# Four batches of self attention written out one after another, each with its neighbours' projections and output between its steps

## What is computed

```
z  = rmsnorm(layernorm(x)) * ln1
kv_d, q_d = z @ kv_d_w, z @ q_d_w                      # 512 -> 128 each
k  = [kv_d @ k_u_w | rope(z @ rope_k_w)]               # 16 heads of 16 + 16
q  = [q_d @ q_u_w  | rope(q_d @ rope_q_w)];  v = kv_d @ v_u_w
P  = softmax(q k^T / sqrt(32), causal)                 # per head, 512 x 512
h  = layernorm(x) + (P v) @ o_w
hn = rmsnorm(h) * ln2
logits = hn @ router_w + router_b                      # 7 experts, the best 2
sum  table <- x + h                                    # written to DRAM, like hn ("rows")
slot table <- token and weight at each chosen expert's next places
```

## Time and profile before

| | |
|---|---|
| Median of 3 runs | 2096.5 us (2091.77 to 2099.65) |
| The profiled execution | 2092.79 us |
| Its span, first to last instruction | 2091.0 us |
| Mean granted TensorE clock | 0.875 |
| TensorE busy | 1733.6 us, 83% |
| VectorE, ScalarE, GpSimd busy | 65%, 50%, 43% |
| `front` without `cross` | about 95 to 791 us |

### The profile page before, as it was taken

One profiled execution on the slowest core, in us unless ns is written; L12 is line 12 of the kernel. 1 busy time (PEld: TensorE's weight loads), 2 busy tenths in 40 slices (PEclk: granted clock), 3 DMA queues, 4 the chain that ended last, 5 costly groups with the idle time before them and its releaser, 6 DMA issues. The chain is left out here.

```text
span 2091.0 us, 34098 instructions
## 1 busy us (share of the span) xinstructions
PE 1733.6 (83%) x9086; PEld 1287.2 (62%) x9087; DVE 1355.9 (65%) x2635; ACT 1037.8 (50%) x1967; POOL 900.1 (43%) x655
## 2 busy tenths in 40 slices
PE   4589879887988984999994794079999999999992
PEld 3456556564655653776772673068888888778881
DVE  6645525544635544667775655069999999899992
ACT  1144234324414423666661110068888888888880
POOL 5100110001011012244441377747888888887881
PEclk9599979988989986999996555579999999999996
DMA  8000000010010016357556213248788888898778
GB/s 293 0 1 1 21 22 2 1 41 3 1 41 1 1 41 172 102 140 181 104 89 183 81 42 90 55 113 203 162 190 195 173 174 190 200 230 198 129 126 271
DMA packets 128910, 222.88 MB, mean 107 GB/s; under 512 B 17536, under 2 KB 60416, under 8 KB 127072
## 3 DMA queue, kind: packets, MB, share of 16 engines
q0 software_dynamic: 52624, 113.84, 28.0%
q1 hardware_dynamic: 76176, 107.71, 15.8%
HBM read 143.74 MB, written 84.18 MB: 109 GB/s over the span
## 5 line engine op out<-in xcount | busy, mean ns | idle before, releaser
L1300 DVE TENSOR_TENSOR moe_w_lo<-moe_w_up,moe_w_hi 128x1536 fp32r<-128x1536 f32 (+1 forms) x216 | 408.4, 1891 | 35.1 <-ACT moe_w_hi L1186 34.4
L1186 ACT ACTIVATE moe_w_hi<-moe_w_up 128x1536 fp32r (+3 forms) x216 | 343.2, 1589 | 19.1 <-SPq L1088 19.1
L1127 POOL DMA_INDIRECT moe_rows<-moe_rows,moe_ids x200 | 319.4, 1597 | 68.1 <-issue 56.7
L1395 PE MATMUL psum<-moe_w_hi,moe_rows_hi 128*128 128x384 f32 (+1 forms) x864 | 323.4, 374 | 16.7 <-DVE moe_rows_lo L1294 16.7
L1396 PE MATMUL psum<-moe_w_lo,moe_rows_hi 128*128 128x384 f32 (+1 forms) x864 | 304.4, 352 | 0.0
L1397 PE MATMUL psum<-moe_w_hi,moe_rows_lo 128*128 128x384 f32 (+1 forms) x864 | 304.2, 352 | 0.0
L1421 PE MATMUL psum<-moe_w_down,moe_hid_t 128*128 (+1 forms) x544 | 268.7, 592 | 1.8 <-DVE moe_tail_t L1288 1.2
L599 POOL TENSOR_TENSOR prob<-x_sb,v_sb 128x512 f32<-128x512 f32 x16 | 20.2, 1265 | 475.2 <-DVE v_sb L738 475.2
L1143 POOL DMA_INDIRECT moe_sum<-moe_res,moe_ids x100 | 165.0, 1650 | 98.5 <-ACT moe_res L1223 55.1
L1143 POOL DMA_INDIRECT moe_other<-moe_res,moe_ids x100 | 165.9, 1659 | 89.3 <-ACT moe_res L1223 34.1
L851 PE MATMUL psum<-k_t,q_t 128*128 128x512 f32 (+3 forms) x512 | 184.2, 471 | 21.1 <-issue 15.8
(11 more groups left out here) (263 smaller groups left out, 3129.1 us busy)
## 6 DMA issues: line engine op xcount, KB each, us to landing
moe_w_up<-in_L_ffn_w_gate SPq DMA_DIRECT2D x32, 384.0 KB, 4.6
moe_w_up<-in_L_ffn_w_up SPq DMA_DIRECT2D x32, 384.0 KB, 5.8
moe_w_down<-in_L_ffn_w_down SPq DMA_DIRECT2D x32, 256.0 KB, 6.2
moe_w_down<-in_L_ffn_w_down SPq DMA_DIRECT2D x64, 128.0 KB, 6.6
moe_sum<-prob SPq DMA_DIRECT2D x4, 1024.0 KB, 4.2
moe_rows<-prob_t SPq DMA_DIRECT2D x4, 1024.0 KB, 4.5
moe_rows<-moe_rows POOLq DMA_DIRECT2D x16, 256.0 KB, 7.1
moe_other<-moe_res POOLq DMA_DIRECT2D x16, 256.0 KB
```

What stands on the lines that cost most here:

```text
L1127: pool.indirect_dma_start(rows[u][:, :], None, d["rows"], bass.IndirectOffsetOnAxis(ids[:, t:t + 1], 0)).then_inc(gathered[u], 16)
L1186: sc.activation(w_hi[u % SPLITS][:, :], w_up[:, bass.ds(at * DC, DC), :].rearrange("p a n -> p (a n)"), ACT.Copy).then_inc(T["wh"], 1)
L1300: v.tensor_tensor(w_lo[u % SPLITS][:, :], w_up[:, bass.ds(at * DC, DC), :].rearrange("p a n -> p (a n)"), w_hi[u % SPLITS][:, :].bitcast(F ...
L1395: mm(ps[:, 2 + i, 0:2 * I], hi, w_h, start=(k == 0), stop=False)
```

## The change

Loops are gone: every stream is written out for all four batches, with one running step number n = 32 b + s. Queries, keys, values and attended results have two sets of buffers (b % 2); `h` has its own memory, and x + h is written over x. The first norm is computed two batches ahead, in steps 24 to 27, and again in part at the residual. `attention` of b now has at each of its steps a piece of `between(b, s)`: norm turns, down, plain, rotary and value projections of batch b+1, and output, second norm, hidden turns, logits, choice and slots of batch b-1. For this `QUERY_ORDER` is (1, 0, 3, 2): the first 16 steps are narrow. A narrow step's two scores share one bank (0 or 1), so banks 2, 3 and 5 are free for the pieces. The queries are stored like the keys, q_t[128, 4, 512]; a head's score contracts over its own 32 rows, and both heads of a step now lie in the same group of 32. In `attend` the loop over heads is the outer one. ScalarE copies q (one pass instead of four), k and q_d, the latter two from VectorE. `take` waits until the bank's former content has been read. Cut to its core:

```diff
-QUERY_ORDER = (3, 0, 2, 1)
+QUERY_ORDER = (1, 0, 3, 2)
...
+        ends = lambda n: STEPS[n % NS][1] == HEADS // 2 - 1
+        is_wide = lambda n: STEPS[n % NS][0] >= 2
+        nth = lambda i: QUERY_ORDER.index(i)
+        BANK = {"zt": (2, 5, 2, 5), "kvd": 2, "qd": 5, "v": (2, 2, 2, 5), "pp": (5, 5, 2, 5), "hnt": (5, 2, 5, 2),
+                "tq": (5, 5, 2, 2), "tk": (2, 2, 5, 5)}
+
+        def head(hp, e):
+
+            return GH * (2 * (hp // GH) + e) + hp % GH
+
+        def score_at(n, e, cols):
+
+            u = n % 2
+            return ps[:, 2 * u + e, 0:cols] if is_wide(n) else ps[:, u, e * 256:e * 256 + cols]
...
+            def take(bank, name, n):
+
+                if bank in emptied:
+                    pe.wait_ge(S[emptied[bank][0]], emptied[bank][1])
+                emptied[bank] = (name, n)
 
...
+            def scores(n):
+                b, s = divmod(n, NS)
+                i, hp = STEPS[s]
+                cols = (i + 1) * P
+                if s == 0:
+                    pe.wait_ge(S["qts"], TPB * (b + 1))
+                    pe.wait_ge(S["kts"], TPB * (b + 1))
+                if s == 1 and n >= NS:
+                    pe.wait_ge(S["pexp"], 2 * (n - 3) + 2)
+                elif n >= 2 and not is_wide(n):
+                    pe.wait_ge(S["pexp"], 2 * (n - 2) + 2)
+                for e in range(2):
+                    if is_wide(n):
+                        if not is_wide(n - 1):
+                            pe.wait_ge(S["pexp"], 2 * (n - 2 + e) + 2)
+                        elif not is_wide(n - 2):
+                            take(2 + e, "pexp", 0)
+                        else:
+                            pe.wait_ge(S["pexp"], 2 * (n - 2) + e + 1)
+                        emptied[2 * (s % 2) + e] = ("pexp", 2 * n + e + 1)
+                    k, g = divmod(head(hp, e), GH)
+                    rows = slice(g * HD, (g + 1) * HD)
+                    mm(score_at(n, e, cols), q_ts[b % 2][rows, k, i * P:(i + 1) * P], k_ts[b % 2][rows, k, 0:cols], start=True, stop=False)
+                    mm(score_at(n, e, cols)[:, cols - P:cols], ident16[:, :], future16[:, :], start=False, stop=True).then_inc(S["st"], 1)
+
+            def attend(n):
+                b, s = divmod(n, NS)
+                (i, hp), u = STEPS[s], s % 2
+                if s == 0:
+                    pe.wait_ge(S["vs"], TPB * (b + 1))
+                pe.wait_ge(S["pta"], n + 1)
+                if i >= 2:
+                    pe.wait_ge(S["ptb"], b * wide_steps(NS) + wide_steps(s + 1))
+                if hp == 0:
+                    other = {1: 3, 0: 2, 3: 1, 2: 0}[i]
+                    if nth(i) >= 2:
+                        pe.wait_ge(S["attd"], b * TPB + nth(other) + 1)
+                    elif b > 0:
+                        pe.wait_ge(S["attd"], (b - 1) * TPB + nth(other) + 1)
+                for e in range(2):
+                    k, g = divmod(head(hp, e), GH)
+                    cols = slice(head(hp, e) * HD, (head(hp, e) + 1) * HD)
+                    for j in range(i + 1):
+                        last = mm(ps[g * HD:(g + 1) * HD, 6 + i % 2, k * P:(k + 1) * P], v_sbs[b % 2][:, j, cols],
+                                  prob_t[:, u, 2 * j + e, :], start=(j == 0), stop=(j == i))
+                last.then_inc(S["pv"], 1)
+
...
-                    for j in range(i + 1):
-                        for e in range(2):
-                            k, g = (2 * hp + e) // GH, (2 * hp + e) % GH
-                            cols = slice((2 * hp + e) * HD, (2 * hp + e + 1) * HD)
-                            last = mm(ps[g * HD:(g + 1) * HD, 6 + i % 2, k * P:(k + 1) * P], v_sb[:, j, cols],
-                                      prob_t[:, u, 2 * j + e, :], start=(j == 0), stop=(j == i))
-                    last.then_inc(S["pv"], 1)
...
+            def output(b, n):
+                t = QUERY_ORDER[n]
+                pe.wait_ge(S["attd"], b * TPB + n + 1)
+                take(3, "hres", b * TPB + n + 1)
...
+            def ranks(b):
+                pe.wait_ge(S["masked"], b + 1)
+                take(3, "slotted", b + 1)
...
+            def between(b, s):
+
+                done, then = b - 1, b + 1
+                if then < BATCH and s in (0, 1):
+                    z_flip(then, 2 * s)
+                    z_flip(then, 2 * s + 1)
+                if done >= 0:
+                    if s in (0, 1, 2):
+                        output(done, s)
+                    if s == 5:
+                        output(done, 3)
+                if then < BATCH:
+                    if s == 3:
+                        down(then, w_kvd, "kvd", "kvds", BANK["kvd"])
+                    if s == 4:
+                        down(then, w_qd, "qd", "qds", BANK["qd"])
+                    if s in (6, 7):
+                        plain(then, s - 6)
+                        turned(then, s - 6)
+                    if s in (5, 6, 7):
+                        values(then, s - 5)
+                if done >= 0:
+                    if s == 9:
+                        logits(done, 0)
+                        logits(done, 1)
+                    if s in (8, 9):
+                        hidden_flip(done, 2 * s - 16)
+                        hidden_flip(done, 2 * s - 15)
+                    if s == 10:
+                        logits(done, 2)
+                        logits(done, 3)
+                if then < BATCH:
+                    if s in (8, 9):
+                        queries_flip(then, s - 8)
+                    if s in (8, 10):
+                        keys_flip(then, (s - 8) // 2)
+                    if s == 10:
+                        values(then, 3)
+                    if s in (11, 12):
+                        plain(then, s - 9)
+                        turned(then, s - 9)
+                if done >= 0 and s == 14:
+                    ranks(done)
...
+            scores(0)
+            scores(1)
+            for n in range(ALL + 2):
+                turning = n + 2 < ALL and is_wide(n + 2) and not is_wide(n)
+                if n + 2 < ALL and not turning:
+                    scores(n + 2)
+                if n >= 2 and ends(n - 2):
+                    denominators(n - 2)
+                if 1 <= n <= ALL:
+                    attend(n - 1)
+                if n < ALL:
+                    pe.wait_ge(S["pexp"], 2 * n + 2)
+                    flip_probs(n)
+                    between(n // NS, n % NS)
+                if turning:
+                    scores(n + 2)
+            for n in range(TPB):
```

More of the change, by code:

```diff
@@ new lines, in _ @@
+            dve.wait_ge(S["zeroed"], 1)
+            for b in range(2):
+                for t in range(TPB):
+                    normed(b, t)
+            for t in range(TPB):
+                rotate(0, t)
+            maxima(0)
+            for n in range(ALL + 2):
+                if n + 1 < ALL:
+                    maxima(n + 1)
+                if 1 <= n <= ALL:
+                    prob_t_first(n - 1)
+                if n >= 2 and ends(n - 2):
+                    attended(n - 2)
+                if 1 <= n <= ALL:
+                    if ends(n - 1):
+                        denominators(n - 1)
+                    between((n - 1) // NS, (n - 1) % NS)
@@ L832, in _ @@
+            for n in range(TPB):
+                residual(LAST, n)
+            second_norm(LAST)
+            hidden(LAST)
+            for part in range(4):
+                route(LAST, part)
         @block.tensor
@@ new lines, in z_flip, with down @@
+            def z_flip(b, t):
+                pe.wait_ge(S["z"], b * TPB + t + 1)
+                take(BANK["zt"][t], "zts", b * TPB + t + 1)
+                four(BANK["zt"][t], z[:, t, :]).then_inc(S["zt"], 1)
+            def down(b, w, name, out, bank):
+                pe.wait_ge(S["zts"], TPB * (b + 1))
+                take(bank, out, b + 1)
+                for k in range(DC):
+                    last = mm(ps[:, bank, :], w[:, k, :], z_t[:, k, :], start=(k == 0), stop=(k == DC - 1))
+                last.then_inc(S[name], 1)
@@ new lines, in hidden_flip, with logits @@
+            def hidden_flip(b, t):
+                pe.wait_ge(S["hn"], b * TPB + t + 1)
+                take(BANK["hnt"][t], "hnts", b * TPB + t + 1)
+                four(BANK["hnt"][t], h[:, t, :]).then_inc(S["hnt"], 1)
+            def logits(b, t):
+                pe.wait_ge(S["hnts"], b * TPB + t + 1)
+                if t == 0:
+                    take(3, "lgs", b + 1)
+                for k in range(DC):
+                    last = mm(ps[:, 3, t * 8:t * 8 + MOE0.routed], hn_t[:, t % 2, k, :], w_rt[:, k, :], start=(k == 0), stop=(k == DC - 1))
+                last.then_inc(S["logit"], 1)
@@ new lines, in _ @@
+            for t in range(TPB):
+                z_flip(0, t)
+            down(0, w_kvd, "kvd", "kvds", BANK["kvd"])
+            down(0, w_qd, "qd", "qds", BANK["qd"])
+            for t in range(TPB):
+                plain(0, t)
+                turned(0, t)
```

(16 more changed lines are left out.)

579 lines of the change are left out of this document (270 added, 309 removed).

## The result

The changed kernel takes 2163.95 us (median of 4 runs, 2163.4 to 2167.8) and the one before, timed with it, 2098.07 (2091.8 to 2100.7): a ratio of 1.0322 [1.0295, 1.0349], slower. The forecast was 2116 and its range ended at 2142, so the side was right and the size was not.

What follows compares the result with a forecast made beforehand. TensorE bounds attention; chains, half clock and a loop end bound the stretches between. Attention work 466.8, moved work 146.4 and waits 27.9 make 641.1 us against 616.7; with ends -0.9, 2092.8 becomes 2116, range 2052 to 2142.

Steps and rivals of the forecast that it cites:

- part 2: In `attend`, both heads of a step share one group, so records run one by one: 17.4 us per batch, 70 in all.
- part 3: Around each head's 32-row score, changes of the array's rows cost 0.22 us an excursion, two per step: 56 us in all.
- part 4: Waits in the stretch: 22 us new, 3.4 at the last attention's end, 2.5 for half clock at attention's start.
- Part 1: Work between attentions moves beside attention: 146.4 us at full clock replaces 226.7, saving 80.3; VectorE and ScalarE don't become the bound.
- Rival C: In `attend`, the heads of a step overlap all the same: 70 us less, 2046; chance 0.07.
- Rival B: Row changes around each head's score cost nothing: 56 us less, 2060, faster; chance 0.27.
- rival D: In steps 5 to 12, VectorE's queue delays the probabilities and `attend` holds TensorE: +30 us, 2146; chance 0.12.
- rival E: In attention, TensorE's clock falls under 32-row scores and 32-column attends; half the work at 1.2 GHz gives about 2350; chance 0.06.
- Part 5: Ends: prologue about 3.5 us shorter; epilogue 2.6 longer, three outputs each waiting 0.85 on shared bank 3.

Runs made afterwards that it cites:

- Run 1: The kernel before, with each head's score contracting over its own 32 rows of padded queries and keys, not all 128: 2483.39 against 2126.22, 1.168.

## Where the prediction held, and where it failed

The stretch was forecast at 641.1 us and measured at 682.9. Of the 41.8 between, the terms below explain 36.5.

| Term of the sum | forecast | measured | difference |
|---|---|---|---|
| Heads in series (part 2) | 70 | 68 | -2 |
| Row changes (part 3) | 56 | 66 | +10 |
| Waits in the stretch (part 4, 22 + 3.4) | 25.4 | 13.6 | -12 |
| Half clock (part 4, start of attention only) | 2.5 | 43 | +40.5 |

(Where the remaining 5 lie is not shown; the projections and turns, priced from short stretches of rows, are the terms left.)

**Part 1 was right.** The projections, norms and routing vanish among the steps, the loop's idle time is gone, and neither VectorE nor ScalarE became the bound. The overlap removed 67 us of waiting. Its saving of 80.3 priced all moved work at full clock, though, and that holds only if the half clock vanishes, which it did not (part 4).

**Part 2 was right**, by place and size: 1.87 us for the 1.9 forecast, `attend` 164.7 us of turns for 87.5 before, of which 10 are the clock's. Its records start one by one, 0.109 us apart. The experiments divide it: a third for the loop order, two thirds for the group. Rival C falls.

**Part 3 was right in its mechanism and too low in size**: 0.26 us an excursion, not 0.22, and not only at the entry and the exit: both records of a score are longer too. The rule of the Trainium skill, TensorEngine Tiling (Array Packing), Key Properties, is that a change of mode drains TensorE; the trace now agrees with it for changes of rows too, at 0.26 us an excursion. Rival B, which had 0.27, falls.

**Part 4 failed.** It took waits that cost 13.6 as 25.4, and rival D falls: a middle batch has 2.7 us of idle time, where D's sign was over 15, and VectorE's release of `attend` (L748) comes to 7.9 us in all, 1.4 in each of the first three batches and 3.7 in the last. (The range was not built as said: it was to hold most of D, whose own time of 2146 lies above its end of 2142.) The step that failed is the clock: the sum has half clock only at the start of attention, at 2.5 us, and the first sign in the prediction's last paragraph says that there is no stretch of it from the first attention to the last output. There are 99 us of it, which cost 43. About 90 of them lie around the turns from narrow to wide steps, in every batch (in the last, from 18 us ahead of the turn). The only reasoning given stands under rival E, that attention now "holds full clock" and does so "with the same idle shares", which takes idle time as the cause. Run 1 shows that cause wrong: the same steps, no more idle than before, lose the clock altogether when the score uses 32 rows. Rival E named that mechanism, but as all or nothing (half of attention, 2350 us, 0.06); here it was in between, and between E and the forecast there was no case. Without the 40.5 us the stretch would have taken 682.9 - 40.5 = 642.4, within 2 us of the forecast, but partly by luck, since the error of part 3 and that of the waits cancel. What in the records lowers the clock stays open; the rows at 391 and 708 us and run 1 show that it falls and stays down without idle time.

**Part 5.** The prologue gained 0.5 us (136.3) and not 3.5. The epilogue is as forecast, 3 us longer, with a wait of 0.94 ahead of each of the last three output tiles in TensorE's timeline, two of them here (what follows `front` takes 2 us more, for which no cause is shown):

```profile
823.78 3.67 PE L1027 MATMUL psum<-w_o,att_t 128*128 128x512 f32 x8 [0.94 <-DVE h L803]
828.39 3.67 PE L1027 MATMUL psum<-w_o,att_t 128*128 128x512 f32 x8 [0.94 <-DVE h L803]
```

## What to carry to other kernels

When work is moved to fill an engine, check first what the new layout does to the instructions that already fill it: here the overlap removed 67 us of waiting, and the head order and the row slices that came with it cost 134. Put operands of neighbouring small products into different row or column groups (and banks) and issue them without a full-array product between, so that they run side by side; with that, the same overlap gives 0.962 instead of 1.032. Do not book half-clock time as saved because its work is moved and the waits around it go: here 111 us of it became 99 in other places, while idle time fell from 81 to 14 us.

## What the runs showed of the hardware that was not expected

- In the changed kernel the granted clock fell from 1.00 to 0.51 behind 8 us in which TensorE was busy for 8.00, and in run 1 it stayed at 0.50 through 188 us in which TensorE was 97% busy. Scores of 32 rows were there each time. In the kernel before they gave 0.50 together with side-by-side `attend`s, 0.83 to 0.85 with serial ones, and 0.85 to 0.95 when the scores ran side by side too; padded to 128 rows, 0.96 to 0.98. The rule behind these numbers is not shown.
- Two edits that each slow a kernel (1.168 and 1.014) gave less together than the first alone: 1.065.
- Two 32-row scores of 512 columns take 1.06 us, the time of one.
- Records in two column groups overlap wherever they are neighbours, also at the seam of two series: 1.46 us for 16 records instead of 1.87, and 0.57 instead of 0.99 for 8, as short as alternating ones (0.56).
- Leaving the hardware loop is worth 0.992 by itself.
